# Fourth routed net's rows gathered, turned and added inside the state-space layer's first body; counter steps of missing products moved to SyncE's queue

## The chip, the cores and the metric

One Trainium2 chip, one core of it. The metric is the device time of one execution of the whole program, in microseconds (us). Three runs of the kernel before gave 2538.24 us (median; 2537.16 to 2541.52).

## The reference, cut to what matters

Two blocks, each with its own modulation vectors, run over `x` of 8 batches x 256 tokens x 128 channels.

```python
h = _layernorm(x) * (1 + ca) + sa
x = x + ga * _L0_attn_ref(h, ...)          # 8 heads, rms-normed, rotated
h = _layernorm(x) * (1 + cb) + sb
x = x + gb * _L0_ffn_ref(h, ...)           # four hard-routed nets q, k, v, f
h = _layernorm(x) * (1 + ca1) + sa1
x = x + ga1 * _L1_attn_ref(h, ...)         # state-space layer: project, convolve, scan, gate, project
h = _layernorm(x) * (1 + cb1) + sb1
x = x + gb1 * _L1_ffn_ref(h, ...)          # 6 layers of windowed attention + gated MLP

def _fff(x, nw, nb, w1, b1, w2, b2, act):  # one hard-routed net
    node = 0                                # 8 binary decisions give each token one of 256 leaves
    ...
    h = act(x . w1[leaf] + b1[leaf])        # 16 hidden values
    return h . w2[leaf] + b2[leaf]
def _forward(x, ...):
    q, k, v = _fff(xn, ...), _fff(xn, ...), _fff(xn, ...)
    y = xn + softmax(q k^T / sqrt(D)) v
    return y + _fff(y, ...)                 # the fourth net, f
```

## The kernel before, in words

Five stages follow one another: a prologue, `attention0`, `routed0`, `mamba1` and `local1`. Each has blocks in which the five engines run their own instruction streams, and between two blocks all of them meet at a barrier. `x` stays in SBUF for the whole program, channels on the partitions, as `xT` (128 x 2048); `cols(b)` are the 256 columns of batch `b`, NB = 8, NT = 2 tiles of 128 tokens in a batch.

**Banks and jobs.** Every product of TensorE goes to one of 8 PSUM banks. `plan` (or `order` in `local1`) lists, for one iteration, which product (`"mean"`, `"WO"`, ...) takes which bank in which order, and each bank has two counters, filled and drained. A product may start when the bank's drained counter has reached all jobs before it. The loops are software pipelines: a body computes the front of batch `it`, the middle of `it - 1` and so on, so that in the first and the last bodies some products do not exist. The counters must move on all the same. `skip` does that: it waits until the bank is free for that job and increments filled and drained by one each. In `attention0` and `local1`, TensorE's own stream does it, with `pe.drain()` first (per product in `attention0`, L289 to L293; once per call, for all the names of a call, in `local1`, L2140 to L2146). `mamba1` skips on TensorE without a drain.

**routed0.** Tokens of a net are scattered by leaf into a buffer of rows in HBM; 12 windows of 512 rows per net go through SBUF (`step`), and window results go back to HBM (`outs_q<-win_out`, SP queue). `gather(n)` on POOL (L1176 to L1186) waits for the last of them and fetches each token's row by 16 indirect DMAs of 128 rows. For the fourth net the rows land in `work_b`; TensorE turns them with 16 transposes into four banks (`FT0` to `FT3`, L1053 to L1060), VectorE adds each bank to `tokens` (the buffer `A`, which holds the transposed `y`; L1434) and adds the sum, times the modulation's column 5, to `xT` (L1437). The block and its barrier end after that. The nodes of the fourth net are decided after `node_ready` (L1426), and VectorE's part of its steps follows.

**mamba1.** `body(0, front)`, a loop over pairs of batches, and `body(NB, mid)`. A front computes `mean` (L1633), `center`, `var` (L1639), `by_root`, the projections `X1` and `XA` (L1647, L1653), `XD` (L1661) and `DT` (L1668), splits B and C into parts (`first_rest` L1895, `second_rest` L1899) and then `steps` (L1904) and the products of B and C (L1677). SP's queue loads `local1`'s first weights (`first.load`) at the start.

**local1.** L1 = 6 layers x 8 batches, N = 48 iterations: `body(0, front)`, `body(1, front, mid)`, a loop over 2 to 47, `body(N, mid, late)`, `body(N + 1, late)`. A front computes queries, keys and values (`Z` L2153, `T` L2164, `V` L2196), a mid the windowed attention (L2177, L2185, L2207, L2217) and the output projection `WO` (L2248), a late the gated MLP (L2256, L2263, L2274, L2283). SP's queue runs `layer(l, ...)`, which loads weights and per iteration shares the values (`Vw<-Vs`, four DMAs, L2099), and after the last layer stores `out_xT` in three parts (L2135), each after a step of `final`.

## Time and profile before

| what | value |
|---|---|
| median of 3 runs | 2538.24 us (2537.16 to 2541.52) |
| time of the profiled execution | 2538.2 us |
| its span, first to last instruction | 2536.3 us |
| instructions | 92155 |
| busy: PE / DVE / ACT / POOL | 2244.7 / 1970.5 / 1752.2 / 1515.5 us |
| mean granted TensorE clock | 0.952 |
| routed0 ends, mamba1 starts (barrier) | 656.45 us |
| local1's loop of 46 iterations | from 1058 us to about 2465 us |

The profiled execution agrees with the median to 0.04 us. PE is TensorE's matmul stream, PEld its weight loads, DVE VectorE, ACT ScalarE, POOL GpSimd, SP SyncE; PEq and SPq are the sequencers or queues of an engine. The granted clock is a share of full speed: 1.00 is 2.4 GHz, 0.50 is 1.2 GHz, and a value between them is a mix of the two over the stretch.

### The profile page before, as it was taken

Reading aid. Unit: us, or ns where it says so; the run is one execution under the profiler, and the core shown is the slowest. Engines: PE = TensorE matmul, PEld = TensorE weight load, DVE = VectorE, ACT = ScalarE, POOL = GpSimd, SP = SyncE. Lnnn points to the kernel's source line nnn. Section 1 sums busy time; section 2 is a strip of 40 time slices with the busy share of each in tenths; the row PEclk is TensorE's granted clock in tenths of the full one; section 3 lists DMA queues with packets and bytes.
Section 4 is the critical chain, followed back from the end, with each engine's and each line's share of the span. In section 5 each row is a group of like instructions: output and inputs, shape, how many; then the busy total and the mean of one; then the engine's idle time right before and its main releaser. Section 6 shows DMA issues by size and latency. Waiting matters only on the chain.

```text
span 2536.3 us, 92155 instructions
## 1 busy us (share of the span) xinstructions
PE 2244.7 (89%) x34780; PEld 1588.3 (63%) x34780; DVE 1970.5 (78%) x3242; ACT 1752.2 (69%) x3580; POOL 1515.5 (60%) x1115
## 2 busy tenths in 40 slices
PE   6999749957477776799999999999999999999995
PEld 4666428745244443477777777777777777777774
DVE  6888666554488887788888888888888888888883
ACT  4777524433477675678888887788778888888773
POOL 2666334340345444667777777777777777777770
PEclk9999979978689898899999999999999999999997
DMA  9300017813200000111211121112211211121111
GB/s 321 95 0 0 22 59 215 260 33 106 71 1 0 0 0 1 36 34 33 58 50 33 33 58 50 33 36 67 55 33 33 66 42 33 40 60 42 33 33 34
DMA packets 128650, 140.03 MB, mean 55 GB/s; under 512 B 10240, under 2 KB 96704, under 8 KB 127552
## 3 DMA queue, kind: packets, MB, share of 16 engines
q1 hardware_dynamic: 124480, 130.69, 18.6%
q0 software_dynamic: 4096, 8.40, 1.1%
q8 instruction: 41, 0.67, 0.1%
q14 instruction: 33, 0.27, 0.0%
HBM read 59.89 MB, written 27.26 MB: 34 GB/s over the span
## 4 chain that ended last, share of the span: by engine, by line
PE 56%; issue 2%; PEld 1%; ACT 1%; DVE 0%; PEldq 0%; POOL 0%; POOLq 0%; DVEq 0%; ACTq 0%
PE ps L2153 13%; PE ps L2164 7%; PE ps L2196 6%; PE ps L2248 6%; PE ps L2217 5%; PE ps L2274 5%; PE ps L2185 5%; PE ps L2207 3%; PE ps L2283 3%; PE ps L2177 1%; PE ps L2263 1%; PE ps L2256 1%; ACT Y L1531 0%; PEld ps L2248 0%; PEld ps L2217 0%
## 5 line engine op out<-in xcount | busy, mean ns | idle before, releaser
L2551 POOL TENSOR_TENSOR c<-a,bq 128x1024 f32<-128x1024 f32 x192 | 454.5, 2367 | 236.3 <-DVE bq L2648 236.1
L2561 POOL TENSOR_TENSOR qn<-c,ss 128x1024 f32<-128x1024 f32 x192 | 378.4, 1971 | 28.4 <-issue 3.2
L2153 PE MATMUL ps<-wqk,xs 128*128 128x512 f32 x768 | 372.6, 608 | 10.1 <-POOL xs L2544 8.2
L2647 DVE TENSOR_TENSOR a<-ps,tab 128x512 f32<-128x512 f32 x384 | 263.1, 685 | 9.8 <-ACT sq L2358 4.6
L2648 DVE TENSOR_TENSOR bq<-ps,tab 128x512 f32<-128x512 f32 x384 | 261.6, 681 | 0.0
L2569 POOL TENSOR_TENSOR z<-z,sm 128x1024 f32<-128x1024 f32 x96 | 182.8, 1904 | 122.6 <-DVE sm L2676 122.6
L1614 POOL TENSOR_TENSOR hC<-hs,Cs 128x1024 f32<-128x1024 f32 x64 | 150.3, 2354 | 174.1 <-ACT Cs L1766 92.2
L2655 DVE TENSOR_REDUCE ss<-sq 128x16 f32<-128x1024 f32 x192 | 230.3, 1217 | 21.7 <-issue 10.9
L2358 ACT ACTIVATE sq<-ps 128x512 f32<-128x512 f32 x384 | 215.4, 597 | 33.8 <-PE ps L2153 33.7
L2153 PEld LDWEIGHTS ps<-wqk,xs 128*128 128x128 f32 x768 | 140.6, 193 | 136.1 <-issue 129.6
L2164 PEld LDWEIGHTS ps<-ident,qn 128*128 128x128 f32 x1536 | 176.0, 141 | 66.6 <-issue 46.4
L2164 PE MATMUL ps<-ident,qn 128*128 128x128 f32 x1536 | 201.8, 274 | 6.1 <-PEq L2146 3.7
L2196 PE MATMUL ps<-wv,xs 128*128 128x512 f32 x384 | 189.4, 595 | 1.0 <-PEq L2146 1.0
L2248 PE MATMUL ps<-oT,wo 128*128 128x256 f32 x768 | 176.6, 384 | 3.6 <-PEq L2146 3.6
L2375 ACT ACTIVATE qT<-ps 128x512 f32<-128x512 f32 x192 | 104.2, 595 | 97.7 <-PE ps L2164 97.7
L2217 PEld LDWEIGHTS ps<-pT,Vw 32*64 32x64 f32 x12288 | 140.0, 130 | 46.8 <-issue 41.0
L2674 DVE TENSOR_REDUCE sm<-z 128x16 f32<-128x1024 f32 x96 | 117.1, 1220 | 55.9 <-ACT z L2389 40.9
L1922 DVE TENSOR_TENSOR_SCAN hs<-dA,ps 128x1024 f32<-128x1024 f32 x64 | 146.4, 2287 | 15.7 <-issue 11.9
L2248 PEld LDWEIGHTS ps<-oT,wo 128*128 128x128 f32 x768 | 144.1, 193 | 22.0 <-issue 3.7
L2217 PE MATMUL ps<-pT,Vw 32*64 32x64 f32 (+1 forms) x12288 | 151.9, 230 | 5.8 <-issue 3.2
L516 POOL TENSOR_TENSOR cq<-a,bq 128x512 f32<-128x512 f32 x64 | 81.8, 1278 | 121.8 <-DVE bq L573 121.8
L1687 PE MATMUL ps<-hC,ident 128*128 128x512 f32 x256 | 137.5, 675 | 13.3 <-POOL hC L1614 13.1
(353 smaller groups left out, 5268.9 us busy)
## 6 DMA issues: line engine op xcount, KB each, us to landing
Vw<-Vs SPq DMA_DIRECT2D x192, 256.0 KB, 4.0
win_rows<-rows_q SPq DMA_DIRECT2D x24, 256.0 KB, 3.5
outs_q<-win_out SPq DMA_DIRECT2D x24, 256.0 KB, 2.4
wqk<-in_wqkv SPq DMA_DIRECT2D x6, 1024.0 KB, 5.1
leaves<-in_q_w SPq DMA_DIRECT2D x1, 4608.0 KB, 20.6
leaves<-in_k_w SPq DMA_DIRECT2D x1, 4608.0 KB, 16.4
leaves<-in_v_w SPq DMA_DIRECT2D x8, 576.0 KB, 6.9
leaves<-in_f_w SPq DMA_DIRECT2D x8, 576.0 KB
```

The lines of the kernel that those rows point to most:

```text
L2153: nc.tensor.matmul(jobs.out(n), xs[:, t * 128:(t + 1) * 128], wqk[:, (2 * y + s) * 512:(2 * y + s + 1) * 512], start=True, stop=True).then ...
L2164: last = nc.tensor.transpose(jobs.out(n)[:, i * 128:(i + 1) * 128], src, core.ident[:, :])
L2196: nc.tensor.matmul(jobs.out(n), xs[:, t * 128:(t + 1) * 128], wv[:, j * 512:(j + 1) * 512], start=True, stop=True).then_inc(jobs.sem_fille ...
L2217: last = nc.tensor.matmul(jobs.out(n)[64 * half:64 * half + 64, a * T + q0:a * T + q0 + qw], Vw[r:r + W, v // 2, h, :], pT[r:r + W, h, q0: ...
L2248: last = nc.tensor.matmul(jobs.out("WO")[:, 0:T], wo[:, i, :], oT[:, i, :], start=(i == 0), stop=(i == H1 // 2 - 1))
L2358: nc.scalar.activation(sq[:, y, :, s, :], heads_view(jobs.out(n)), ACT.Square).then_inc(sq_ready.sem, 1)
L2551: nc.gpsimd.tensor_tensor(f(c), f(a), f(bq), ALU.add).then_inc(c_ready.sem, 1)
L2561: nc.gpsimd.tensor_tensor(qn[:, t, y, :, :, :].rearrange("p h s e -> p h (s e)"), c[:, y, :, :, :].rearrange("p h s e -> p h (s e)"), spre ...
L2569: nc.gpsimd.tensor_tensor(z[:, t, :, :], z[:, t, :, :], spread(sm[:, t, :], 2 * W, 2), ALU.mult).then_inc(weights_ready.sem, 1)
L2647: nc.vector.tensor_tensor(a[:, y, :, s, :], Zs, spread(table(0, s), H1), ALU.mult)
L2648: nc.vector.tensor_tensor(bq[:, y, :, 1 - s, :], Zs, spread(table(1, 1 - s), H1), ALU.mult)\
L2655: nc.vector.tensor_reduce(ss[:, y, :], sq[:, y, :, :, :].rearrange("p h s e -> p h (s e)"), axis=AX.X, op=ALU.add)\
```

## The change

1. The fourth net's return path leaves `routed0`. Its 16 gathers are issued on POOL in `mamba1`'s block, after POOL's memsets. `y` (in `tokens`) times the modulation is added to `xT` already in `routed0`, right after `node_ready`. In `mamba1`'s first body the rows of batch `b` are turned by TensorE (`turn_rows(b)`, two transposes) and VectorE adds them times the modulation (`finish_rows(b)`): batch 0 ahead of `mean`, the others between the pieces of the front. `work_b`, `slot` and the semaphores of the window stores and of the rows move to `Core`, since both stages use them. SP waits for all the rows before it loads `local1`'s weights.
2. `pe.drain()` leaves `attention0`'s `skip`.
3. `local1`'s `skip` moves from TensorE to SP's queue, without a drain: the missing products of iteration 0 and `WO` of iteration 1 before the first layer, the rest of iteration 1 after iteration 0's values are shared, those of N and N + 1 after the last layer, before the stores.

```diff
@@ attention0, pe @@
                 def skip(name, it):
-                    pe.drain()
                     pe.wait_ge(*jobs.free(it, name))
@@ routed0, plan and pe @@
-        plan += [(f"FT{g}", g, 1) for g in range(NG4)]
...
-                pe.wait_ge(fetched[3], 16 * NTILE)
-                for g in range(NG4):
-                    pe.wait_ge(*free(f"FT{g}"))
-                    for j in range(4):
-                        last = nc.tensor.transpose(out(f"FT{g}")[:, tile(j)], got[3][:, 4 * g + j, :], core.ident[:, :])
-                    last.then_inc(sem_filled(f"FT{g}"), 1)
@@ routed0, pool @@
                 scatter(3, False)
-                gather(3, False)
@@ routed0, dve @@
                 dve.sem_inc(node_ready, 1)
+                for b in range(NB):
+                    nc.vector.scalar_tensor_tensor(x[:, cols(b)], A[:, cols(b)], core.mod[0][:, 5, b:b + 1], x[:, cols(b)], ALU.mult, ALU.add)
                 for t in range(S1, S1 + WG + 4):
                     step(t, S1, S1 + WG)
                 core.scan_weights.taps_and_rows(core, dve)
-                for g in range(NG4):
-                    dve.wait_ge(*filled(f"FT{g}"))
-                    nc.vector.tensor_tensor(A[:, c512(g)], out(f"FT{g}"), A[:, c512(g)], ALU.add).then_inc(sem_drained(f"FT{g}"), 1)
-                    dve.drain()
-                    for b in (2 * g, 2 * g + 1):
-                        nc.vector.scalar_tensor_tensor(x[:, cols(b)], A[:, cols(b)], core.mod[0][:, 5, b:b + 1], x[:, cols(b)], ALU.mult, ALU.add)
@@ mamba1 @@
+        turn_in = lambda b: core.banks.ps[:, (7, 0, 1)[b % 3], 0:T]
             def _(sp):
+                for b in range(NB):
+                    sp.wait_ge(core.row_in[b], 2 * 16 * NT)
                 first.load(sp)
...
+                for j in range(NOUTS):
+                    pool.wait_ge(core.win_out[j], 16 * (WG // NOUTS) * 4)
+                for i in range(NTILE):
+                    nc.gpsimd.indirect_dma_start(f_rows[:, i, :], None, core.routed_outs[:, :],
+                                                 bass.IndirectOffsetOnAxis(ap=core.slot[:, 3, i:i + 1], axis=0))\
+                        .then_inc(core.row_in[i // NT], 16)
...
+                def turn_rows(b):
+                    pe.wait_ge(core.row_in[b], 2 * 16 * NT)
+                    if b >= 3:
+                        pe.wait_ge(finished, b - 2)
+                    for j in range(NT):
+                        last = nc.tensor.transpose(turn_in(b)[:, j * 128:(j + 1) * 128], f_rows[:, NT * b + j, :], core.ident[:, :])
+                    last.then_inc(turned, 1)
...
+                def finish_rows(b):
+                    dve.wait_ge(turned, b + 1)
+                    nc.vector.scalar_tensor_tensor(x[:, cols(b)], turn_in(b), core.mod[0][:, 5, b:b + 1], x[:, cols(b)], ALU.mult, ALU.add)
+                    dve.drain()
+                    dve.sem_inc(finished, 1)
@@ local1, sp @@
+                def skip(it, front, mid, late, names):
+                    on = {FRONT: front, MID: mid, LATE: late}
+                    for part, n, _ in order:
+                        if n in names and not on[part]:
+                            sp.wait_ge(*jobs.free(it, n))
+                            sp.sem_inc(jobs.sem_filled(n), 1)
+                            sp.sem_inc(jobs.sem_drained(n), 1)
...
                         share_values(l * NB + b)
+                        if first and b == 0:
+                            skip(1, True, True, False, ALL[1:])
...
+                skip(0, True, False, False, ALL)
+                skip(1, True, True, False, ALL[:1])
                 layer(0, True, False)
                 with sp.Fori(1, L1 - 1) as l:
                     layer(l, False, False)
                 layer(L1 - 1, False, True)
+                skip(N, False, True, True, ALL)
+                skip(N + 1, False, False, True, ALL)
@@ local1, pe @@
-                def skip(names, it):
-                    pe.drain()
-                    for n in names:
-                        pe.wait_ge(*jobs.free(it, n))
-                        pe.sem_inc(jobs.sem_filled(n), 1)
-                        pe.sem_inc(jobs.sem_drained(n), 1)
...
                         if part:
                             op(it, *args)
-                        else:
-                            skip(names, it)
```

TensorE's order at the end of `routed0` and the start of `mamba1` was this before (L983 and L986 are the last window, `ident,work_b` the transposes of the gathered rows, L1633 on is `mamba1`; `l0f_fetched3` counts the gathers):

```order
L986 MATMUL ps<-work_c,win_hid 128x128 x4
L1060 MATMUL ps<-ident,work_b 128x128 [waits drained0,l0f_fetched3]
L1060 MATMUL ps<-ident,work_b 128x128 x3
L1060 MATMUL ps<-ident,work_b 128x128 [waits drained1]
L810 UNCONDITIONAL_BRANCH
L1622 UNCONDITIONAL_BRANCH [waits barrier_Pool_Activation_PE_DVE_SP_release]
L1633 MATMUL ps<-xT,mean_w 128x256 [waits drained2]
L1639 MATMUL ps<-lsq,mean_w 128x256 [waits drained7,drained3,drained2,drained5,l1a_squared]
```

Of the changed kernel, at the same place:

```order
L987 MATMUL ps<-work_c,win_hid 128x128 x4
L811 UNCONDITIONAL_BRANCH
L1626 UNCONDITIONAL_BRANCH [waits barrier_Pool_Activation_PE_DVE_SP_release]
L1641 MATMUL ps<-ident,work_b 128x128 [waits l0f_row_in0]
L1641 MATMUL ps<-ident,work_b 128x128
L1646 MATMUL ps<-xT,mean_w 128x256 [waits drained2,l0f_finished]
L1652 MATMUL ps<-lsq,mean_w 128x256 [waits drained7,drained3,drained2,drained5,l1a_squared]
L1641 MATMUL ps<-ident,work_b 128x128 [waits l0f_row_in1]
L1641 MATMUL ps<-ident,work_b 128x128
L1660 MATMUL ps<-h,win 128x256 [waits drained4,drained6,drained5,l1a_h_ready]
```

All the transposes have moved behind the barrier, two ahead of the mean and two behind the variance here, and the mean now waits for VectorE's first addition.

VectorE's order in the first body now is this (L1914 with `ps` is the addition of turned rows, L1920 and L1925 center and scale, L1931 and L1935 the two rests, L1940 the steps):

```order
L1907 UNCONDITIONAL_BRANCH [waits barrier_Pool_Activation_PE_DVE_SP_release]
L1914 SCALAR_TENSOR_TENSOR xT<-ps,mod,xT 128x256 [waits l0f_turned]
L1920 TENSOR_TENSOR cent<-xT,ps 128x256 [waits filled2]
L1925 TENSOR_TENSOR cent<-ps,cent 128x256 [waits l1a_scaled]
L1914 SCALAR_TENSOR_TENSOR xT<-ps,mod,xT 128x256 [waits l0f_turned] x3
L1931 TENSOR_TENSOR ps<-ps,parts 32x256 [waits l1a_part1]
L1914 SCALAR_TENSOR_TENSOR xT<-ps,mod,xT 128x256 [waits l0f_turned]
L1935 TENSOR_TENSOR ps<-ps,parts 32x256 [waits l1a_part2]
L1914 SCALAR_TENSOR_TENSOR xT<-ps,mod,xT 128x256 [waits l0f_turned] x3
L1940 TENSOR_TENSOR dt<-u,e 128x512 [waits l1a_soft]
```

The eight additions stand between the five operations that were there alone before.

In `local1`'s last body (N + 1) TensorE's order was this before (`drained0` to `drained7` are the banks' counters, and a wait for many of them ahead of a product is that of the skipped products ahead of it):

```order
L2248 MATMUL ps<-oT,wo 128x256 [waits drained5,drained4,drained7,drained3,drained1,l1f_mid_weights]
L2248 MATMUL ps<-oT,wo 128x256 x7
L2256 MATMUL ps<-Y,mean_w 128x256 [waits drained3,drained2,drained7,drained0,drained1]
L2263 MATMUL ps<-lsq,mean_w 128x256 [waits drained6,drained3,drained5,drained4,drained0,l1f_squared]
L2274 MATMUL ps<-cent,w 128x256 [waits drained1,drained5,drained7,drained3,drained6,drained0,drained2,drained4,l1f_xn,l1f_late_weights]
```

And in the changed kernel:

```order
L2303 MATMUL ps<-oT,wo 128x256 [waits drained1,l1f_mid_weights]
L2303 MATMUL ps<-oT,wo 128x256 x7
L2311 MATMUL ps<-Y,mean_w 128x256 [waits drained1]
L2318 MATMUL ps<-lsq,mean_w 128x256 [waits drained0,l1f_squared]
L2329 MATMUL ps<-cent,w 128x256 [waits drained5,l1f_xn,l1f_late_weights]
```

The waits of the skipped products are gone from TensorE; they now stand on SP's queue ahead of the first store of `out_xT`.

## Rows read from the trace of the kernel before

**Rows 1.** Busy time by stretch: us, PE, PEld, DVE, ACT, POOL, PEclk, DMA share, GB/s.

```profile
626.00:656.50 30.50, 3.47 (x17) 3.26 (x17) 6.02 (x12) 0.03 (x1) 15.19 (x17) 0.58 0.12 35
...
1058.00:2465.00 1407.00, 1404.26 (x29077) 1021.35 (x29078) 1205.08 (x1877) 1127.63 (x2340) 1024.97 (x687) 1.00 0.18 44
...
2500.00:2536.00 36.00, 17.39 (x168) 12.09 (x166) 6.90 (x15) 7.85 (x13) 0.00 (x0) 0.67 0.03 8
```

**Rows 2.** Timeline, end of routed0: start, duration, work, idle before it and releaser.

```profile
625.80 0.23 ACT L1469 ACTIVATE A<-A 128x32 f32<-128x32 f32 x1
627.27 0.97 POOL L1182 DMA_INDIRECT work_b<-outs_q,slot  x1 [57.20 <-DMA outs_q<-win_out]
...
646.04 0.94 POOL L1182 DMA_INDIRECT work_b<-outs_q,slot  x1 [0.30 <-issue]
648.55 3.46 PE L1060 MATMUL ps<-ident,work_b 128*128 128x128 f32 x16 [25.06 <-DMA work_b<-outs_q,slot]
...
655.22 0.88 DVE L1437 SCALAR_TENSOR_TENSOR xT<-tokens,mod,xT 128x256 f32<-128x256 f32 x2
...
656.49 1.19 PE L1633 MATMUL ps<-xT,mean_w 128*128 128x256 f32 x2 [4.48 <-PEq L810]
```

**Rows 3.** Busy time, 505 to 527 us: 16 earlier gathers on POOL; columns as in rows 1.

```profile
505.00:527.00 22.00, 17.71 (x96) 14.37 (x96) 11.49 (x32) 12.87 (x35) 15.27 (x16) 0.92 0.18 51
```

**Rows 4.** Timeline, VectorE, the stretch ahead of the fourth net's windows.

```profile
576.73 0.75 DVE L1358 TENSOR_SCALAR win_node<-ps,node_thr 128x512 bf16<-128x512 f32 x1 [20.67 <-PE ps L957]
```

**Rows 5.** Timeline, mamba1's first body.

```profile
663.85 4.34 PE L1653 MATMUL ps<-h,wtap 128*128 128x256 f32 x16
...
669.13 1.10 PE L1661 MATMUL ps<-xs,wx 128*96 128x256 f32 x4 [0.93 <-ACT xs L1788]
...
675.17 0.69 DVE L1904 TENSOR_TENSOR dt<-u,e 128x512 f32<-128x512 f32 x1 [2.66 <-ACT e L1817]
...
675.63 1.46 PE L1677 MATMUL ps<-parts,sel_b 96*128 96x256 bf16 x6 [3.69 <-ACTq L1804]
```

**Rows 6.** Timeline, end of attention0.

```profile
293.20 0.72 POOL L532 TENSOR_TENSOR acc<-acc,Ot 128x256 f32<-128x256 f32 x1 [1.16 <-DVE Ot L594]
...
296.64 0.66 PE L370 MATMUL ps<-ident,acc 128*128 128x128 f32 x2 [4.29 <-PEq L293]
```

**Rows 7.** TensorE's waits, 0 to 50 us: total, times, longest.

```profile
PE ps L329 <- PEq L293: 2.7, 3, 1.3
```

**Rows 8.** Timeline, TensorE, mamba1's last body: two skips stand ahead of this.

```profile
976.38 1.88 PE L1687 MATMUL ps<-hC,ident 128*128 128x512 f32 x4
```

**Rows 9.** Timeline, local1's iteration 0.

```profile
1000.83 1.90 POOL L2561 TENSOR_TENSOR qn<-c,ss 128x1024 f32<-128x1024 f32 x1
...
1005.69 1.06 PE L2164 MATMUL ps<-ident,qn 128*128 128x128 f32 x8 [3.68 <-PEq L2146]
```

**Rows 10.** Timeline, local1's body N (first row) and last body.

```profile
2474.56 3.69 PE L2248 MATMUL ps<-oT,wo 128*128 128x256 f32 x16
...
2501.06 1.58 PE L2217 MATMUL ps<-pT,Vw 32*64 32x64 f32 x128 [0.82 <-PEq L2146]
...
2502.74 2.06 ACT L2420 ACTIVATE oT<-ps 128x512 f32<-128x512 f32 x4 [4.84 <-PE ps L2217]
...
2506.28 6.47 PE L2248 MATMUL ps<-oT,wo 128*128 128x256 f32 x16 [3.64 <-PEq L2146]
...
2514.26 0.67 PE L2256 MATMUL ps<-Y,mean_w 128*128 128x256 f32 x2 [1.50 <-PEq L2146]
...
2516.51 1.19 PE L2263 MATMUL ps<-lsq,mean_w 128*128 128x256 f32 x2 [1.58 <-PEq L2146]
...
2519.26 0.60 ACT L2442 ACTIVATE cent<-cent,par 128x256 f32<-128x256 f32 x1 [0.55 <-DVE cent L2689]
2522.09 4.54 PE L2274 MATMUL ps<-cent,w 128*128 128x256 f32 x12 [4.40 <-PEq L2146]
...
2528.77 2.70 PE L2283 MATMUL ps<-hid,w 128*128 128x256 f32 x6 [2.13 <-PEq L2146]
```

More of the change, by code:

```diff
@@ L105, in __init__ @@
         self.one = self.sem("one")
+        self.f_rows = self.sb(ctx, "work_b", [128, NB * T])
+        self.slot = self.sb(ctx, "slot", [128, 4, NT * NB], mybir.dt.uint32)
+        self.win_out = [self.sem(f"l0f_win_out{j}") for j in range(4)]
+        self.row_in = [self.sem(f"l0f_row_in{b}") for b in range(NB)]
     def sb(self, ctx, name, shape, dt=F32):
@@ L715, in routed0 @@
         sb = lambda *a: core.sb(ctx, *a)
-        A, Bf, Cf = (sb(n, [128, NTOK]) for n in ("tokens1", "work_b", "work_c"))
+        A, Bf, Cf = sb("tokens1", [128, NTOK]), core.f_rows, sb("work_c", [128, NTOK])
         xtok = sb("xtok", [128, NTILE, D])
@@ L754, in routed0 @@
         centered, squared, scaled, h_ready, xn_ready, xt_ready = (sem(n) for n in ("centered", "squared", "scaled", "h", "xn", "xt"))
-        slot_ready, v_in = sem("slots"), [sem(f"v_in{b}") for b in range(NB)]
-        scattered, fetched, staged = [sem(f"scattered{n}") for n in range(4)], [sem(f"fetched{n}") for n in range(4)], sem("spares_staged")
-        win_in, win_out = [sem(f"win_in{j}") for j in range(NROWS)], [sem(f"win_out{j}") for j in range(NOUTS)]
+        slot_ready, v_in = sem("slots"), core.row_in
+        scattered, fetched, staged = [sem(f"scattered{n}") for n in range(4)], [sem(f"fetched{n}") for n in range(2)], sem("spares_staged")
+        win_in, win_out = [sem(f"win_in{j}") for j in range(NROWS)], core.win_out
         qk_ready, mx_ready, e_ready, P_ready, PT_ready, y_ready, yt_ready = (sem(n) for n in ("qk", "mx", "e", "P", "PT", "y", "yt"))
@@ L1584, in mamba1 @@
         first = core.local
+        turned, finished = core.sem("l0f_turned"), core.sem("l0f_finished")
+        f_rows = core.f_rows[:, :].rearrange("p (i e) -> p i e", e=D)
+        turn_in = lambda b: core.banks.ps[:, (7, 0, 1)[b % 3], 0:T]
         with nc.Block() as block:
@@ L1710, in do_over @@
                             do(part, (n,), over_channels, n, new if part_of[n] == FRONT else old)
+                    begin = not mid
+                    if begin:
+                        turn_rows(0)
+                        pe.wait_ge(finished, 1)
                     do(front, ("mean",), mean)
@@ L1715, in body @@
                     do(front, ("var",), variance)
+                    if begin:
+                        turn_rows(1)
                     do(mid, (), over_states, b, 1)
@@ L1719, in body @@
                     do(front, ("X1", "XA"), project)
+                    if begin:
+                        turn_rows(2)
+                        turn_rows(3)
                     do_over(mid, "B6")
                     do(front, ("XD",), to_dbl, xs)
+                    if begin:
+                        turn_rows(4)
                     do(front, ("DT",), to_dt)
+                    if begin:
+                        turn_rows(5)
+                        turn_rows(6)
+                        turn_rows(7)
+                        pe.wait_ge(finished, NB)
                     do_over(mid, "C5")
@@ L1941, in body @@
                     old_xs, old_sres, old_du = xs2[:, 1 - y, :, :], sres2[:, 1 - y, :, :], du2[:, 1 - y, :, :]
+                    begin = not mid
+                    if begin:
+                        finish_rows(0)
                     if mid:
@@ L1950, in body @@
                         by_root(it)
+                    if begin:
+                        for n in (1, 2, 3):
+                            finish_rows(n)
                     if mid:
@@ L1958, in body @@
                         first_rest(it, parts)
+                    if begin:
+                        finish_rows(4)
                     if mid:
@@ L1962, in body @@
                         second_rest(it, parts)
+                    if begin:
+                        for n in (5, 6, 7):
+                            finish_rows(n)
                     if mid:
@@ L2070, in local1 @@
         jobs = Jobs(core.banks, [(n, b, 1) for _, n, b in order], N + 2)
+        ALL = ["WO"] + [n for _, n, _ in order if n != "WO"]
         heads_view = lambda ap: ap.rearrange("p (h e) -> p h e", e=EH)
```

6 lines of the change are left out of this document (3 added, 3 removed).

## The prediction

> **What bounds the kernel now.** I read the table of busy time by stretch first. From 1058 to 2465 us TensorE is busy 1404.26 of 1407.00 us at a granted clock of 1.00 [rows 1]. Nothing in the diff touches that loop's products, so it passes a shift through and gives nothing itself. What the change can win lies where TensorE waits: the stretch 626 to 656.5 us, in which it works 3.47 of 30.5 us, and the last 36 us, in which it works 17.39 us [rows 1]. The timeline then says what it waits for in each. I work against the profiled execution's own 2538.2 us, which is the median's 2538.24; the difference between them is nothing.
>
> **1. The rows' return, 626 to 656.5 us.** ScalarE ends the windows' side at 625.80 + 0.23 = 626.03; the store of the last window lands at 627.27, when POOL starts its first gather; the sixteenth starts at 646.04, so one comes every (646.04 - 627.27) / 15 = 1.25 us. TensorE starts the transposes at 648.55, 2.51 us after the last issue; of these 0.94 is the instruction, 1.57 what follows it. VectorE's last addition ends at 656.10, and the mean of `mamba1` starts at 656.49 [rows 2]. The chain is store, 16 gathers, 16 transposes, additions, barrier, mean.
>
> In the changed kernel the barrier follows 626.03; the old one cost 656.49 - 656.10 = 0.4 us, so it opens at about 626.4, and POOL's memsets (0.6 us in all) end at about 627.1, before the store lands. The first gather stays at 627.3. Batch 0 needs two: issued at 628.5, landed 2.5 us later at 631.1. Two transposes (3.46 / 16 = 0.22 each, up to 0.6 together with the first one's fill), one addition (0.44, half of 0.88 [rows 2]) and about 0.1 of hand-over each put the mean at 632.35. **Gain 24.1 us** (22 to 25).
>
> The fourteen other gathers then run beside the front. Batch b is in at 627.27 + 1.25 (2b + 1) + 2.51, so 638.5 for batch 3 and 648.5 for batch 7. The front shifted by 24.1 reads [rows 5]: tap products end 644.1, `XD` 645.0, `steps` 651.1, products of B and C 651.5. `turn_rows(1..4)` find their rows long there. Four transposes between the taps and `XD` take 0.9 of the 0.93 that TensorE waits for ScalarE; I allow 0.3. Batch 7 lands at 648.5, is turned by 649.1 and added by 649.7, ahead of 651.1 and 651.5: hidden, with 1.4 us of slack. From 651.5 on the order is the old one. On SP, the first weights of `local1` are issued at about 648.6 instead of 656.5; they are needed after 1000.
>
> The eight additions of `y` moved to `routed0` cost 8 x 0.44 = 3.5 us on VectorE, which has nothing to do for 20.67 us ahead of the fourth net's first step, waiting for TensorE [rows 4]. They are issued after `node_ready`, so TensorE doesn't wait for them: 0. Without that cover they would cost 3.5 us.
>
> **2. attention0 without drains.** In the last body `acc` is ready at 293.92; TensorE starts its transposes at 296.64, after 4.29 us attributed to its own sequencer, over 11 skips: 0.39 each [rows 6]. Skips without a drain are nearly free: in `mamba1` two of them stand ahead of the product at 976.38, and it has no idle time in front [rows 8]. So the start follows `acc` by 0.1: 2.6 us. The last iterations' other skips give another 0.3. At the front, three waits of 2.7 us together (the longest 1.3) stand on the same sequencer [rows 7]; part of them only waits for data, and I take 1.5. **Gain 4.4 us** (3 to 5).
>
> **3. local1's skips on SP.** *Iteration 0.* `qn` is ready at 1002.73 and TensorE starts at 1005.69, 3.68 us of sequencer idle over ten names, 0.37 each [rows 9]. It could start at 1002.85, 2.84 earlier. What follows on VectorE waits for TensorE's products, so I take 2.8, and 0.6 for the skips of iteration 1. **Gain 3.4 us** (2 to 4.5).
>
> *The tail.* The last body is a chain with one engine at a time. Products wait 0.82, 3.64, 1.50, 1.58, 4.40 and 2.13 us for the sequencer [rows 10]. A part of each is the other engine's work. `WO` starts 1.48 us after ScalarE's `oT` ends (2502.74 + 2.06 = 2504.80, to 2506.28), `L2274` starts 2.23 us after ScalarE's `cent` ends at 2519.86; with 0.08 us of hand-over 1.4 and 2.15 can be saved. I halve the first (0.7), since its skips are few. By the same reading VectorE's and ScalarE's work leaves 0.5, 0.45 and 0.95 us at `L2256`, `L2263` and `L2283`, and the 0.82 goes nearly whole (0.75). That is 5.5; body N has one such stall of 0.6 on its path. **Gain 6.1 us** (4.5 to 8.5).
>
> The new skips on SP stand behind four DMA issues of 3.2 us at 2472.6 and each waits for a bank. TensorE's first product that could need one comes at 2478.1; SP is there at 2475.8. The first store of `out_xT` now also waits for them. It was issued 38 us before the end and now goes about 5 us before the last; it takes under 4 us, so 0, with +1 as its bound. One register instruction more in the loop of 46 iterations is hidden behind a full array (2.74 us of idle time in 1407 [rows 1]): 0, between -1.5 and +1.5.
>
> **The sum.** 24.1 - 0.3 + 4.4 + 3.4 + 6.1 = 37.7 us; 2538.2 - 37.7 = **2500.5 us**. The low ends of the gains give 22 + 3 + 2 + 4.5 = 31.5, with +1 and +1.5 against it 29, so 2509; the high ends give 25 + 5 + 4.5 + 8.5 = 43, so 2495.
>
> **A rule against the row.** Sixteen gathers of the earlier nets, from 505 to 527 us, took 15.27 us of POOL, 0.95 each, while VectorE was busy 11.49 of the 22 us [rows 3]: VectorE beside them did not stretch them. The Trainium skill, "SBUF — State Buffer", section "SBUF: two separate sides", says that a DMA issued from GpSimd's queue stalls while VectorE runs an operation in a two-port mode, since its descriptors can't be written. By that rule the gathers beside the front, whose cover in the old kernel was an idle VectorE, would come slower; by the row the cost is 0.
>
> **Rivals.**
> - *The gathers slow down beside the front*, and batch 7 holds the products of B and C (10%). For: they ran beside idle engines before, and the front loads from all sides. Against: [rows 3]. With a slack of 1.4 us over 15 intervals it decides from 1.34 us each; at 1.6 us the last lands 5.3 us later, 3.9 us past the cover: 2504.4.
> - *The skips on SP arrive late or the waits were ScalarE's and VectorE's anyway* (15%): the gains of local1 shrink from 9.5 to 2 or 3 us. For: the first 1.4 at `WO` is not explained by its few names. Against: 0.37 us per name, the same in both stages. 2507.5.
> - *The last stretch keeps the high clock* (15%). `WO` takes 6.47 us there for 16 products [rows 10], at a stretch's mean clock of 0.67 [rows 1]; the same 16 products in body N, right behind busy work, took 3.69 [rows 10]. With less idle time ahead of it the clock may not have fallen by then: -2.8, so 2497.7. Against: 3.6 us of idle time shrink only to 2.2, and the last 36 us stay mostly idle. The Trainium skill, "TensorE: Matmul & The Clock Gate", section "What's actually happening", says that the gate sets the clock by how busy the array has been recently. By that rule a stretch with fewer pauses runs faster; the row above agrees in its sign.
> - *Slower than before* (1.5%). The counters' steps of the last iterations and of the loop share SP with the shared values, and the loop body's addresses have moved. If each of the 46 iterations became longer by 0.82 us (37.7 / 46) the gain would be gone, above 0.93 us the kernel would be slower by more than 0.2%; at 1 us it gives 2500.5 + 46 = 2546.5. Against: in the loop no instruction but one register operation is added, and TensorE is busy 99.8% of it.
> - *The change doesn't do what it says* (1.5%): the mean still waits for most rows, as the barrier or POOL's order hold batch 0 back. Then only 2 and 3 remain and the time is 2524 or more.
>
> **How the numbers follow.** The forecast as summed gets 57%, with 2497.5 to 2504 as its own range. The range for 8 in 10 and some more reaches from 2495 (all gains high, clock kept) to 2509 (low ends, late skips). Within 0.2% (5.1 us, about what a measurement of this kernel can tell from no change) would need a loss of over 32 us somewhere: 1.5%. Slower 1.5%, faster 97%.
>
> **What would show it.** Right: POOL's first gather in `mamba1` at 627.3 and the sixteenth 18.8 us later; the mean at 632 to 633; no wait for rows of batch 7 ahead of the products of B and C at 651.5; the eight additions inside VectorE's idle 20 us; no sequencer wait of 4 us before `L370`'s products; `local1`'s first transposes within 0.2 us of `qn`; in the last body gaps of one hand-over. Wrong: gathers over 1.34 us apart, `finished` as the releaser of the B and C products, products in body N or 1 that wait for SP, a third or more of the tail's stalls still there under another name, or a loop of over 1408 us.

## The result and the profile after

| | before | changed |
|---|---|---|
| median | 2539.88 us (4 runs, 2537.16 to 2545.35) | 2502.95 us (4 runs, 2501.68 to 2506.29) |
| ratio, 95% interval | | 0.9846 (0.9832 to 0.9859) |
| profiled execution / its span | 2538.2 / 2536.3 us | 2506.3 / 2504.4 us |

The forecast was 2500.5 us, the range 2495 to 2509. The medians differ by 36.9 us, the forecast by 37.7. The profiled execution of the changed kernel took longest of its four, and the two profiled spans differ by only 31.9 us, which matters below.

The timeline of the changed kernel, end of `routed0` and start of `mamba1` (start us, duration us, work, idle before it and releaser), answers to [rows 2]:

```profile
623.66 0.23 ACT L1460 ACTIVATE A<-A 128x32 f32<-128x32 f32 x1
...
625.63 0.98 POOL L1601 DMA_INDIRECT work_b<-outs_q,slot  x1 [1.06 <-issue]
...
629.44 0.69 PE L1641 MATMUL ps<-ident,work_b 128*128 128x128 f32 x2 [8.08 <-DMA work_b<-outs_q,slot]
...
630.17 0.49 DVE L1914 SCALAR_TENSOR_TENSOR xT<-ps,mod,xT 128x256 f32<-128x256 f32 x1 [10.34 <-PE ps L1641]
...
630.74 1.22 PE L1646 MATMUL ps<-xT,mean_w 128*128 128x256 f32 x2 [0.61 <-DVEq L1915]
...
644.43 0.95 POOL L1601 DMA_INDIRECT work_b<-outs_q,slot  x1 [0.30 <-issue]
...
646.98 0.20 PEld L1641 LDWEIGHTS ps<-ident,work_b 128*128 128x128 f32 x2 [0.35 <-DMA work_b<-outs_q,slot]
...
647.14 1.69 DVE L1914 SCALAR_TENSOR_TENSOR xT<-ps,mod,xT 128x256 f32<-128x256 f32 x3
...
649.51 0.69 DVE L1940 TENSOR_TENSOR dt<-u,e 128x512 f32<-128x512 f32 x1 [0.68 <-ACT e L1846]
```

The mean starts 5.11 us behind the first gather, where it was 29.22 us before. The sixteenth gather is issued 18.80 us after the first (18.77 before): 1.25 us each. Beside them TensorE is busy for 11.8 of 19.8 us, but VectorE only for 2.8. The last rows are added by 648.83, 0.7 us before `dt`. From the mean to `dt` it is 18.77 us, where it was 18.68: the rows of the other batches cost the front 0.1 us. The first gather starts 1.97 us behind ScalarE's last exponential instead of 1.47: POOL now has its memsets ahead of it, and the store no longer is what it waits for.

The last body of `local1` in the changed kernel, same view, answers to [rows 10]:

```profile
2475.86 2.00 PE L2272 MATMUL ps<-pT,Vw 32*64 32x64 f32 x128
...
2477.96 2.07 ACT L2473 ACTIVATE oT<-ps 128x512 f32<-128x512 f32 x4 [4.53 <-PE ps L2272]
...
2480.17 6.73 PE L2303 MATMUL ps<-oT,wo 128*128 128x256 f32 x16 [2.31 <-ACT oT L2473]
...
2487.94 0.67 PE L2311 MATMUL ps<-Y,mean_w 128*128 128x256 f32 x2 [1.04 <-DVE Y L2759]
...
2489.71 1.22 PE L2318 MATMUL ps<-lsq,mean_w 128*128 128x256 f32 x2 [1.10 <-ACT lsq L2481]
...
2492.50 0.60 ACT L2495 ACTIVATE cent<-cent,par 128x256 f32<-128x256 f32 x1 [0.55 <-DVE cent L2742]
2493.19 4.49 PE L2329 MATMUL ps<-cent,w 128*128 128x256 f32 x12 [2.26 <-issue]
...
2497.86 1.66 PE L2338 MATMUL ps<-hid,w 128*128 128x256 f32 x6 [0.17 <-DVE hid L2751]
```

Each product but `L2329` now names ScalarE or VectorE as its releaser, and each starts a hand-over (0.05 to 0.14 us) behind the work that it needs; `L2329` too, 0.09 us behind ScalarE's `cent`. `L2338` starts even before the last third of `hid`, since nothing stands ahead of it any more, and its six products take 1.66 us instead of 2.70: the granted clock over them is 1.00 here and was 0.54 before.

To tell stages from chance, the same five marks were read in the timeline of every profiled execution (all marks are starts; differences in us): **A** from `routed0`'s first product to ScalarE's last exponential in its block; **B** from there to `mamba1`'s first `dt`; **C** from there to ScalarE's first operation on `local1`'s first batches (`first_root`); **D** from there to the last pair of additions to `xT`. "Start" is when `routed0` begins.

| profiled execution | start | A | B | C | D |
|---|---|---|---|---|---|
| before | 298.4 | 327.4 | 49.4 | 304.2 | 1553.3 |
| before, second one (e11) | 296.5 | 329.6 | 49.7 | 307.8 | 1553.5 |
| changed | 293.4 | 330.2 | 25.9 | 307.4 | 1543.9 |
| changed, second one (e4) | 296.4 | 327.8 | 27.0 | 305.0 | 1544.1 |
| e1 rows only | 297.3 | 331.9 | 25.6 | 303.6 | 1553.8 |
| e2 skips only | 295.0 | 326.0 | 49.2 | 304.0 | 1543.6 |
| e3 no drain, on TensorE | 293.1 | 328.3 | 25.7 | 303.6 | 1540.7 |
| e5 serial rows | 295.3 | 330.3 | 43.0 | 303.7 | 1543.9 |
| e6 hybrid | 294.4 | 332.2 | 26.4 | 305.4 | 1541.3 |
| e7 twelve extra products | 294.1 | 329.8 | 25.9 | 307.3 | 1542.0 |
| e8 hybrid and twelve | 295.5 | 330.2 | 25.9 | 307.3 | 1537.1 |
| e9 six extra products | 293.3 | 328.8 | 25.9 | 307.3 | 1539.4 |
| e10 hybrid and six | 294.3 | 329.2 | 25.8 | 303.7 | 1534.2 |
| e12 probe, two more operations in each front | 294.4 | 329.6 | 25.5 | 310.1 | 1542.9 |

D follows the code and repeats to 0.5 us where `local1`'s code is the same (1553.3, 1553.5 and 1553.8 with the old one; 1543.9, 1544.1, 1543.6 and 1543.9 with the changed one). B does too, but for 26.4 in e6 and 27.0 in e4; in e4 the granted clock over the tap products was 0.64, where the first profile of the same kernel had 0.73. The start and A vary by several us whatever the kernel. C, the probe left out, lies at 303.6 to 305.4 or at 307.3 to 307.8, and both kernels have been seen at either. The 31.9 us between the two first profiles are 5.0 at the start, 23.5 in B and 9.4 in D, less 2.8 in A and 3.2 in C.

### The profile page after: what moved, and what is told of

Its sections match the earlier page's. It is cut to its first block, busy times and chain, and to the rows that moved or that the text cites. A ratio compares the mean times of both kernels' runs of the same rounds, so it can differ in the third digit from the quotient of the medians.

```text
span 2504.4 us, 92187 instructions
## 1 busy us (share of the span) xinstructions
PE 2243.0 (90%) x34780; PEld 1585.7 (63%) x34780; DVE 1976.5 (79%) x3246; ACT 1751.1 (70%) x3580; POOL 1516.9 (61%) x1115
## 4 chain that ended last, share of the span: by engine, by line
PE 58%; issue 1%; ACT 1%; DVE 1%; POOL 0%; POOLq 0%; DVEq 0%; ACTq 0%; SPq 0%
PE ps L2208 13%; PE ps L2219 7%; PE ps L2303 7%; PE ps L2251 6%; PE ps L2272 6%; PE ps L2329 5%; PE ps L2240 5%; PE ps L2262 3%; PE ps L2338 3%; PE ps L2232 1%; PE ps L2318 1%; PE ps L2311 1%; ACT Y L1522 0%; ACT sq L2411 0%; POOL z L2622 0%
```

## The experiments

**The parts alone.** e1 is the kernel before with part 1 (all of the diff's `routed0` and `mamba1`). e2 is the kernel before with parts 2 and 3.

```diff
 e1: attention0 and local1 as before
                 def skip(name, it):
                     pe.drain()
...
 e2: routed0 and mamba1 as before
                 scatter(3, False)
                 gather(3, False)
```

> Part 1 of the change alone (rows gathered, turned and added in the state-space layer's first body); the drains of attention0 and TensorE's skips in local1 are those of before. Theory A (the account by stages): the return path gives 23.5 us and nothing else moves, ratio 0.9907, 2516 us beside 2539.9. Rival B: the 3.2 us that the profile after lost in the state-space loop, in two iterations where dt and du ran beside POOL's hC, belong to this part and come with it every time: 20.5 us, ratio 0.992. In the profile: the mean about 24 us earlier; A expects dt and du at 0.69 us in all iterations, B the two stretched pairs again.

> Parts 2 and 3 alone (no drain in attention0's skips, local1's skips on SP); the fourth net's rows return as before. Theory A: attention0 gives 5 us, local1's front 3.5, its last two bodies 6 to 8: 14 to 16 us, ratio 0.994. Rival B (most of it lost to code loading in the last bodies and to another order of the DMAs in routed0): 8 us, ratio 0.997. In the profile: L370's products 4.5 to 5 us earlier, routed0's end earlier by the same amount by A, by 2 only by B.

e1: 2520.09 us against 2542.99, ratio 0.9910 (0.9892 to 0.9928). e2: 2531.18 us, ratio 0.9944 (0.9919 to 0.9968). The product of the two is 0.9855, the whole change 0.9846: they add. For e1 the times alone can't decide, since the interval holds both theories' ratios (0.9907 and 0.992). The profile does: B fell by 23.8 us, and there was no stretched `dt` or `du` (C is 303.6), so that loss is not tied to part 1. For e2 the ratio is theory A's, but not its share for attention0: `L370`'s products start 1.7 us sooner behind `acc`, where 4.5 to 5 us were expected, and the two medians differ by 11.8 us, not 14 to 16. e2's `routed0` took 326.0 us, the quickest of all: nothing was lost there.

**The drain or the queue.** e3 keeps `local1`'s skips on TensorE, without the drain (the edit against the kernel before is shown).

```diff
                 def skip(names, it):
-                    pe.drain()
                     for n in names:
                         pe.wait_ge(*jobs.free(it, n))
```

> As the changed kernel, but local1's skips stay on TensorE, without the drain. Theory A (the drain was the cost, the counter steps run ahead of the array): within 1 us of the changed kernel, ratio 0.9845. Rival B (each counter step costs TensorE's sequencer 0.24 us, as the 2.63 us over 11 names at the end of attention0 in the profile after say): 35 names on the path in local1 cost some 5 us more than the changed kernel, ratio 0.9865. In the profile: sequencer waits of 0.24 us per name ahead of the last body's products by B, none by A.

2500.64 us beside 2504.47 for the changed kernel (e4); ratio 0.9837 (0.9819 to 0.9855), so the intervals overlap, but D differs by 3.2 to 3.4 us, over six times its scatter of 0.5. Neither theory had this: against skips on TensorE without a drain, SP's queue costs more than it saves. It does save the sequencer's time in the last body. TensorE's waits of e3, 2455 to 2495 us (total, times, longest):

```profile
PE ps L2320 <- PEq L2192: 3.1, 1, 3.1
...
PE ps L2329 <- PEq L2192: 1.5, 1, 1.5
```

These are 2.26 and 0.17 in the changed kernel. Where it loses more shows when D is cut in four: from ScalarE's `first_root` to the loop's first `Z` product, from there to the first values product of body N, from there to the last body's second values product, and the rest.

| | to the loop | loop | body N | last body |
|---|---|---|---|---|
| before | 79.0 | 1412.3 | 30.4 | 31.7 |
| before (e11) | 79.3 | 1411.9 | 30.4 | 31.8 |
| changed | 75.5 | 1412.6 | 30.9 | 24.9 |
| changed (e4) | 75.4 | 1413.9 | 31.6 | 23.2 |
| e3 | 74.3 | 1409.7 | 30.6 | 26.1 |
| e6 hybrid | 75.9 | 1411.2 | 30.5 | 23.7 |

Against the changed kernel, e3 is 1.0 to 1.2 us shorter before the loop and 2.9 to 4.2 in it, and 1.2 to 2.8 longer in the last body. The entry of the loop of 46 iterations, in the changed kernel and then in e3 (timeline, TensorE):

```profile
1031.37 0.92 PE L2272 MATMUL ps<-pT,Vw 32*64 32x64 f32 x67 [1.80 <-issue]
1032.42 3.57 PE L2208 MATMUL ps<-wqk,xs 128*128 128x512 f32 x4
```

```profile
1023.36 1.22 PE L2263 MATMUL ps<-pT,Vw 32*64 32x64 f32 x94 [1.63 <-issue]
1024.99 1.98 PE L2199 MATMUL ps<-wqk,xs 128*128 128x512 f32 x4 [0.41 <-issue]
```

The same four products take 3.57 us in one and 1.98 in the other, at a granted clock of 0.55 and 1.00: low against high. They take 3.45 to 3.68 us in all seven profiles of kernels with every skip on SP (changed, e2, e4, e5, e7, e9, e12), and 1.98 in all four with the first bodies' skips on TensorE and no drain (e3, e6, e8, e10). But the old form with the drain is no better, 3.37, 3.78 and 3.78 us (before, e11, e1). So the change did not bring the low clock to the loop's entry; it kept it, and e3 avoids it. What keeps the clock high there was not tested, and the other 1.3 us or more that e3 wins in the loop have no cause shown.

TensorE also stops in the middle of runs of tiny products, with nothing to wait for. From `first_root` to the end of the loop's first pass, and around body N, the stops over 0.4 us sum to 5.6 us in the kernel before (1.83, 1.43, 0.53 and 1.78) and 6.1 in e11, 9.1 in the changed kernel (0.48, 1.92, 1.80, 1.59, 1.83 and, in body N, 1.49), 9.0 in e4, 6.9 in e3 and 7.1 in e1, whose `local1` is that of before. They sit where code is run for the first time, before the loop, in its first pass and behind it. That they are waits for code is the likely reading, not a tested one. Nor is their sum the loss: e1 has 1.5 us more of them than before, and its D is longer by 0.5.

**A second profile of each kernel.**

> The changed kernel once more, unchanged, for a second profile and more times. If the 2.8 us lost in routed0 and the 3.2 us lost in the state-space loop are fixed by the order, they are there again to 0.3 us; if they are of one execution (DMA landings, phase of the clock), one or both differ, and the span is 2501 or less instead of 2504.4. Ratio 0.9846.

> The kernel before once more, unchanged, for a second profile. In eight profiled executions with part 1, routed0 took 327.8 to 332.2 us from its first product to the last exponential of its block; before it took 327.4. If that is chance (before's one profiled execution was a quick one: 2538.2 where its runs go to 2547), this one has 329 to 331 and a span above 2538. If part 1 stretches routed0 by itself (moved buffers), it has 327.4 or less again.

e4: 2504.47 us, ratio 0.9843 (0.9825 to 0.9861); A is 327.8 and not 330.2, C 305.0 and not 307.4. The span was 2503.9 us all the same, and not 2501 or less, since the start came 3.0 us later and B took 1.1 more. e11: one time, 2542.61 us; A is 329.6, inside the spread of the kernels with part 1, and C 307.8. So neither the 2.8 us "lost" in `routed0` nor the 3.2 us in the state-space loop belongs to the change. The first profiles of the two kernels lie on opposite sides of a chance spread.

**What the two levels of C are.** VectorE and POOL, timeline, in the changed kernel's first profile:

```profile
681.60 2.36 POOL L1618 TENSOR_TENSOR hC<-hs,Cs 128x1024 f32<-128x1024 f32 x1 [6.05 <-PE ps L1700]
682.97 1.53 DVE L1940 TENSOR_TENSOR dt<-u,e 128x512 f32<-128x512 f32 x1
684.66 1.29 DVE L1950 TENSOR_TENSOR ps<-ps,du 128x512 f32<-128x512 f32 x2 [0.16 <-issue]
685.82 2.35 POOL L1618 TENSOR_TENSOR hC<-hs,Cs 128x1024 f32<-128x1024 f32 x1 [1.87 <-ACT Cs L1795]
686.05 2.67 DVE L1944 TENSOR_TENSOR du<-dt,xs 128x512 f32<-128x512 f32 x1
```

And in its second (e4):

```profile
681.86 2.35 POOL L1618 TENSOR_TENSOR hC<-hs,Cs 128x1024 f32<-128x1024 f32 x1 [4.41 <-PE ps L1700]
682.25 2.29 DVE L1958 TENSOR_TENSOR_SCAN hs<-dA,ps 128x1024 f32<-128x1024 f32 x1 [0.29 <-issue]
684.62 0.69 DVE L1940 TENSOR_TENSOR dt<-u,e 128x512 f32<-128x512 f32 x1
...
686.87 0.69 DVE L1944 TENSOR_TENSOR du<-dt,xs 128x512 f32<-128x512 f32 x1
687.47 2.35 POOL L1618 TENSOR_TENSOR hC<-hs,Cs 128x1024 f32<-128x1024 f32 x1 [3.27 <-ACT Cs L1795]
```

`dt` and `du` read both inputs from SBUF, as `hC` does on POOL. Where one starts inside an `hC`, it ends 0.54 us after that ends (682.97 + 1.53 = 684.50; `hC` ended at 683.96). Where it starts first, it takes its usual 0.69 us, and so does `hC` its 2.35 when the two overlap by 0.1 us or less, as here. The scan and the products with `ps` have one input in PSUM and run beside `hC` at their usual length. The probe adds two copies of `du` per front:

```diff
                         scan(it, 0)
+                        steps_by_input(dt, du, xs)
                         input_states(it, 1, du)
+                        steps_by_input(dt, du, xs)
```

> The changed kernel with two extra copies of the product du = dt x xs on VectorE in each front of the state-space layer (same inputs, same result, both inputs in SBUF), one right behind the first scan, one behind the next products of states. Theory A (an operation of VectorE with two SBUF inputs can't run while POOL's hC, which also reads SBUF, is running; who starts first keeps the way): each copy that starts inside an hC ends 0.5 us after it, 1.2 to 2.7 us long, and each that doesn't takes 0.69. Rival B (the stretched pairs in the profile after were something else, such as the clock): copies take 0.69 us wherever they start.

One execution, 2507.97 us. No `dt` and no original `du` was stretched this time. Four of the added copies started inside an `hC`, two of them early enough to last longer. One that didn't and one that did (timeline, VectorE and POOL):

```profile
769.99 2.34 POOL L1618 TENSOR_TENSOR hC<-hs,Cs 128x1024 f32<-128x1024 f32 x1 [2.03 <-PE ps L1700]
772.18 0.69 DVE L1944 TENSOR_TENSOR du<-dt,xs 128x512 f32<-128x512 f32 x1
...
809.32 2.34 POOL L1618 TENSOR_TENSOR hC<-hs,Cs 128x1024 f32<-128x1024 f32 x1 [2.68 <-PE ps L1700]
810.87 1.34 DVE L1944 TENSOR_TENSOR du<-dt,xs 128x512 f32<-128x512 f32 x1
```

`hC` ends at 772.33 and 811.66, the copies at 772.87 and 812.21: 0.54 and 0.55 us later, as in the other two, so the shorter the overlap, the shorter the wait. Theory A holds, though the copies hit fewer `hC` than I had expected. The other order shows too. Here a copy starts 0.05 us before an `hC`:

```profile
657.06 0.69 DVE L1944 TENSOR_TENSOR du<-dt,xs 128x512 f32<-128x512 f32 x1
657.11 2.84 POOL L1618 TENSOR_TENSOR hC<-hs,Cs 128x1024 f32<-128x1024 f32 x1 [11.47 <-ACT Cs L1795]
```

The copy keeps its 0.69 us and `hC` takes 2.84 instead of 2.35. This is the rule of the Trainium skill, "SBUF — State Buffer", section "Who interferes with whom": an operation of VectorE with two SBUF inputs and one of GpSimd that reads SBUF exclude each other, and the second to start waits. The rows agree, in six of thirteen profiles besides the probe, e11 among them, and in the probe in both orders. C goes with the number of stretched operations: 303.6 to 305.0 us in the seven profiles without one, 305.4 with two (e6), 307.3 to 307.8 in the five with four (changed, e7, e8, e9, e11). Four of them (1.53, 2.67, 1.81, 2.37, less 0.69 each) cost 5.6 us on VectorE, and 2.3 to 4.2 on the path by the difference in C.

Whether it happens seems to go back to `hC`'s releaser: `hC` waits for TensorE's products `ps<-hC`. Eight of them take 3.60 us in the first profile of before and in e4, and 4.64 in the changed kernel's first (e11 is like the latter), and then POOL starts later and lands on `dt`. The table by stretch of the changed kernel (us, PE, PEld, DVE, ACT, POOL, PEclk, DMA share, GB/s) has the granted clock at 0.83 there, where the same stretch of the kernel before (696.5 to 706.5 us) has 1.00:

```profile
670.80:680.80 10.00, 8.62 (x30) 5.37 (x30) 8.19 (x9) 8.25 (x16) 3.11 (x2) 0.83 0.00 0
```

That part was read from four executions, not tested.

**All rows ahead of the mean.** e5 takes the overlap out; VectorE's eight additions move ahead of the mean as well.

```diff
                     if begin:
-                        turn_rows(0)
-                        pe.wait_ge(finished, 1)
+                        for n in range(NB):
+                            turn_rows(n)
+                        pe.wait_ge(finished, NB)
                     do(front, ("mean",), mean)
```

> The changed kernel, but the first body turns and adds the rows of all eight batches before its mean, so that nothing of the front runs beside the gathers. Theory A (the gain of part 1 is the front running beside fourteen gathers): the last rows land 2.5 us after the sixteenth issue, 21.3 us after the first gather's start, and the last turn and addition take 0.9 us more, so the mean follows the first gather by 22.2 to 22.5 us instead of 5.1; 17 us slower than the changed kernel, ratio to before 0.9915. Rival B (what helps is the earlier barrier and the removed bank additions, and VectorE beside POOL's gathers costs them time): 10 us slower or less, ratio below 0.989, and the gathers come closer together than 1.25 us.

2523.60 us, ratio 0.9925 (0.9908 to 0.9941). The mean starts at 650.03, 22.55 us behind the first gather at 627.48; B is 43.0 against 25.9, and the gathers still come every 1.25 us. Theory A holds: of part 1's 23.5 us, 17.1 are the front beside the gathers and 6.4 the rest (no bank additions, two transposes instead of sixteen behind the last rows, the barrier ahead; not told apart by a run).

**The better half of both.** e6 puts the skips of 0, 1 and N on TensorE, without a drain, and leaves those of N + 1 on SP.

```diff
 SP:
-                        if first and b == 0:
-                            skip(1, True, True, False, ALL[1:])
...
-                skip(N, False, True, True, ALL)
                 skip(N + 1, False, False, True, ALL)
 TensorE:
                         if part:
                             op(it, *args)
+                        elif front or mid:
+                            skip(names, it)
```

> The changed kernel with local1's skips of iterations 0, 1 and N back on TensorE (no drain) and only those of N + 1 on SP. Theory A (two effects of opposite sign: on SP the first bodies suffer code loading and a clock that falls, 4 to 5 us; in the last body SP saves TensorE's 0.24 us per name, 2.3 us): it has the better half of both, local1 takes 1518.5 us from its first mean to the end less 2.3, ratio 0.983. Rival B (where the code stalls fall is a matter of the code's length alone, not of who skips): local1 within 1 us of the changed kernel's 1523.9, ratio 0.9845.

2499.49 us, ratio 0.9823 (0.9806 to 0.9841). D is 1541.3: 2.6 to 2.8 us less than in the changed kernel, about half of what A expected, and 0.6 more than e3. The loop is entered at the high clock (1.98 us), but one stop of 2.01 us among the scores' products was 0.69 in e3. Part of rival B stays true: where such stops fall changes with the code.

**Filling the last body's gaps.** e7 puts extra products (identity times the loaded weights, read by nobody) into banks of missing products; e9 has half of them; e8 and e10 are e7 and e9 on top of e6.

```diff
+        WARM = [("Z00.0", "Z00.1"), ("T10.1",), ("S1.0",), ("V1", "V2")]
...
+                def warm(it, names):
+                    for n in names:
+                        pe.wait_ge(*jobs.free(it, n))
+                        nc.tensor.matmul(jobs.out(n), core.ident[:, :], wqk[:, 0:512], start=True, stop=True)\
+                            .then_inc(jobs.sem_filled(n), 1)
...
 e7: WARM = [("Z00.0", "Z00.1", "Z01.0", "Z01.1"), ("T10.1", "P0.1"), ("S1.0", "S1.1"), ("V1", "V2", "T01.1", "P1.0")]
```

> The changed kernel with twelve extra products of 512 columns (identity times the loaded query weights, nobody reads them) in the gaps of the last body: four ahead of WO, two ahead of mean, two ahead of var, four ahead of F0; they take banks of missing products, whose counters TensorE then moves. Theory A (the rival on the clock was right in kind: WO at 6.7 us and F0 to F2 at 4.5 us are products at the low clock, because TensorE idled 2.3 us ahead of them): WO takes 3.7 us, F0 to F2 3.5, the end comes 3 to 4 us earlier, ratio 0.983. Rival B (the clock has fallen for longer idle times before, or the extra products are late and hold up the real ones): no change or 1 to 2 us slower, WO above 5 us.

> As the run with twelve extra products, with half of them: two ahead of WO, one ahead of mean, one ahead of var, two ahead of F0 (one takes 0.92 us at the high clock). Theory A (half a gap of work is enough to keep the high clock, and then the real products are no longer held up): from the last body's second values product to the last addition 20.5 us, against 24.9 in the changed kernel and 23.7 with twelve; 4 us below the changed kernel, ratio 0.983. Rival B (the clock falls with half the work): WO at 6 us or more, no gain.

> Both edits together: skips of 0, 1 and N on TensorE without a drain, the twelve extra products in the last body. If both theories A hold, the gains add: 7 to 8 us below the changed kernel, ratio 0.9815, 2494 us. If neither does, 0.9845.

> The six extra products on top of the hybrid of skips (0, 1 and N on TensorE without a drain, N + 1 on SP). Theory A: 7 us below the changed kernel, ratio 0.9812, 1517 us or less from local1's first mean to the end (1523.9 in the changed kernel). Rival B (gains don't add, because the extra products shift the code): 0.9825.

| | median | ratio to before | last values product to last addition |
|---|---|---|---|
| changed (e4) | 2504.47 us | 0.9843 (0.9825 to 0.9861) | 23.2 us (24.9 in the first profile) |
| e7, twelve | 2503.54 us | 0.9840 (0.9821 to 0.9858) | 23.2 us |
| e9, six | 2499.14 us | 0.9826 (0.9813 to 0.9840) | 20.2 us |
| e8, hybrid and twelve | 2498.37 us | 0.9821 (0.9805 to 0.9838) | 22.8 us |
| e10, hybrid and six | 2495.19 us | 0.9812 (0.9799 to 0.9826) | 20.1 us |

The kernel before was measured anew beside some of these, at medians of 2543.0 to 2546.0 us, so the ratios compare better than the medians. TensorE in the last body of e9 (timeline):

```profile
2474.44 1.96 PE L2273 MATMUL ps<-pT,Vw 32*64 32x64 f32 x128
2476.32 1.98 PE L2358 MATMUL ps<-wqk,ident 128*128 128x512 f32 x4
2478.71 3.69 PE L2304 MATMUL ps<-oT,wo 128*128 128x256 f32 x16 [0.40 <-ACT oT L2504]
...
2488.17 2.83 PE L2330 MATMUL ps<-cent,w 128*128 128x256 f32 x12 [0.55 <-issue]
```

`WO` takes 3.69 us and `L2330`'s products 2.83 instead of 4.49, at a granted clock of 1.00. Without extra products `WO` is not the same in every execution. It took 6.73 us in the changed kernel's first profile (granted clock 0.54) and this in its second (0.68), which is most of the 1.7 us between the two in the last column:

```profile
2481.11 5.38 PE L2303 MATMUL ps<-oT,wo 128*128 128x256 f32 x16 [2.32 <-ACT oT L2473]
```

In e7 the two take 3.62 and 2.75 us, but its extra products run 1.2 us into `WO`'s time and 1 us into `F0`'s, and the last body is no shorter than in e4: theory A of e7 holds for the clock and fails for the time. Theory A of e9 holds for both, with 20.2 us against 23.2 to 24.9. e8 is 6.1 us below the changed kernel by the medians, with D 6.8 to 7.0 less, where 7 to 8 were expected. e10 is the fastest kernel of the study, 0.31% below the changed one on the ratios, with D at 1534.2 against 1543.9, which is more than the 7 us that its theory A expected.

## Why the prediction was right, step by step

- **The rows' return**: 24.1 - 0.3 = 23.8 us forecast, B fell by 23.5 (49.4 to 25.9; by 22.7 between the two second profiles). The chain of two gathers, landing, turn, addition, mean was 5.11 us long against 5.1 from the terms. "The first gather stays at 627.3" failed by 0.5 us: POOL reaches it after the barrier and its memsets, 1.97 us behind the exponential, not when the store lands. The slack at batch 7 was 0.7 us and not 1.4.
- **The eight moved additions**: 3.26 us in VectorE's idle time (3.5 forecast), which was still 18.0 us long.
- **attention0**: 4.4 forecast, 2.7 measured. At the end, the time from the start of `acc` to the start of `L370`'s products fell from 3.44 to 1.78 us in every profile without the drain: 1.7 and not 2.6. The step that failed is "skips without a drain are nearly free". With an idle array the sequencer needs 2.63 us for the 11 names, 0.24 each; with the drain it was 0.39. The row from `mamba1` [rows 8] showed two skips under a busy array. The rest gave about 1.1 instead of 1.8, by the mean start of that `acc` over 3 profiles with and 10 without the drains (292.2 and 291.1). Within each group it scatters by 2 to 3 us, so the 1.1 is an estimate and not shown.
- **local1**: 3.4 + 6.1 = 9.5 forecast, D fell by 9.4 in both pairs of profiles. The sum is right partly by luck, for its split is not. Up to the loop 3.5 us were gained, which is the term (3.4; the transposes start 0.05 us behind `qn`). For body N and the first wait of the last body 1.35 (0.6 + 0.75) were forecast; in fact the loop took 0.3 longer and body N 0.5. Behind that, the last body gained 6.75 and not 4.75. Halving the term at `WO` was wrong: it starts 1.34 us sooner behind `oT`, not 0.7. And where 0.95 was forecast at the last six products, 3.05 came: they start with the first third of `hid` rather than behind all of it (2.0), and at a granted clock of 1.00 instead of 0.54 they are 1.04 us shorter. Against this, `oT` starts 0.4 us later behind the values product and `WO` takes 0.26 longer. The split also moves by chance: between the second profiles (e11 and e4) the same four stretches give 4.0, -2.0, -1.2 and 8.6.
- **SP's queue**: no product of TensorE in `local1` has SP's queue as its releaser. The first store of `out_xT`, at 2498.93, goes 2.9 us before the last one and not 5, and was hidden: the last store still goes right behind the last additions.
- **The rivals.** Gathers slowed by VectorE: no, 1.25 us each, but VectorE was busy only 2.8 of their 19.8 us (625.6 to 645.4 us), so this front is a weak test. The rule of the Trainium skill ("SBUF — State Buffer", "SBUF: two separate sides") on descriptors beside two-port operations wasn't seen; whether the front has such operations was not tried. The clock kept high by the change itself: in part. `WO`, on which the rival was built, took 6.73 us and 5.38 in the two profiles, where the rival needed 3.69, but the last six products did run at the high level, and so the sign that the page's rule gives is right there. With its gaps filled `WO` too ran at the high level (e9). Late skips: no. The sum of the measured terms is 23.5 + 2.7 + 9.4 = 35.6 us, against 36.9 by the medians; no run gives a cause for the 1.3 between them.

## What to carry to other kernels

A stage that ends with gathered rows can hand them over by batch, and the next stage's front then hides all but the first: here 17 of 23.5 us. When a drain stands ahead of counter steps, try first the form without it on the same engine: here the move to another queue was 3 us worse, for reasons that only in part are shown. Where one product at a time is on the path, a few unread products that fit into the gaps can shorten the real ones; twice as many held the real ones up and gave nothing. Read at least two profiles of each kernel before a difference of 3 us in one stage is given a cause.

## What the runs showed of the hardware

- VectorE with two SBUF inputs and POOL reading SBUF don't run together: 0.69 us became 1.34 to 2.67, always ending 0.54 to 0.56 us behind POOL's operation, and POOL's 2.35 us became 2.84 where VectorE was first. VectorE's operations with one input in PSUM kept their length beside `hC` (the scan 2.29 us).
- Two executions of the same kernel can fall on either side of this, which made a stage of 304 us longer or shorter by 2.3 to 4.2 us.
- A counter step on TensorE's sequencer with an idle array takes 0.24 us without a drain (2.63 us over 11) and 0.37 to 0.39 with one (4.29 us over 11).
- Behind 2.3 us without a product, `WO`'s 16 products of 128x256 take 5.38 to 6.73 us in the changed kernel's two profiles, at a granted clock of 0.68 to 0.54. Where unread products run in that gap (e9) they take 3.69 us at 1.00.
- 16 indirect gathers of 128 rows from POOL's queue come every 1.25 us, beside idle engines (before) as beside a front in which TensorE is busy 11.8, ScalarE 6.8 and VectorE 2.8 of 19.8 us (changed).
